# All remaining MLP units ahead of the matrix gathers, with four PSUM bank pairs for each kind of work

## The reference, cut to what matters

```python
x = x + gnn(layernorm(x), W, M, src, dst)          # relu(x@W + segment_sum((x@M)[src], dst))
h = (xn @ W_gat).reshape(M, HEADS, NUM_EXPERTS)    # 16 features a node
a_src = (h * att_src).sum(-1); a_dst = (h * att_dst).sum(-1)
e = leaky_relu(a_src[src] + a_dst[dst], 0.2)
ee = exp(e - segment_max(e, dst)[dst])
agg = segment_sum(h[src] * (ee / segment_sum(ee, dst)[dst])[:, :, None], dst)
g = gates(top2(layernorm(agg)))
out = sum_e g[e] * (gelu(xn @ W1[e] + b1[e]) @ W2[e] + b2[e])
```

## Time and profile before

| | |
|---|---|
| median of 3 runs | 3540.27 us (3537.82 to 3543.89) |
| profiled execution, time | 3540.27 us |
| profiled execution, span | 3539.0 us |
| mean granted TensorE clock | 0.882 of full speed |
| busy: PE, PEld | 2560.6, 1708.4 us |
| busy: DVE, ACT, POOL | 2344.6, 920.5, 2377.0 us |

### The profile page before, as it was taken

The page is one execution under the profiler, slowest core; times in us unless marked ns, Lnnn a source line. Parts: engine busy times, 40 slices in busy tenths (PEclk is TensorE's granted clock), DMA queues, the critical chain, the costliest instruction groups (busy, mean ns, idle before and its releaser), DMA issues.

```text
span 3539.0 us, 36336 instructions
## 1 busy us (share of the span) xinstructions
PE 2560.6 (72%) x10290; PEld 1708.4 (48%) x10315; DVE 2344.6 (66%) x5820; ACT 920.5 (26%) x1581; POOL 2377.0 (67%) x2827
## 2 busy tenths in 40 slices
PE   2556777767677777768877887777798787777725
PEld 1334555545555545546555555555554444443314
DVE  6677676776775555565545555555358898899957
ACT  3000111111112222211111111111145565555514
POOL 3666666666656666646666666666788888888841
PEclk9776998989888989889989888989799999999968
DMA  9676566666666666646666666666622122241147
GB/s 287 227 251 205 180 201 186 204 190 196 203 184 194 205 188 204 201 145 211 202 210 196 200 202 213 197 207 207 171 62 55 45 60 57 55 131 43 41 148 230
DMA packets 476775, 600.78 MB, mean 170 GB/s; under 512 B 72486, under 2 KB 415390, under 8 KB 474526
## 3 DMA queue, kind: packets, MB, share of 16 engines
q1 hardware_dynamic: 378766, 375.94, 32.9%
q0 software_dynamic: 97216, 219.88, 22.4%
q10 hardware_dynamic: 592, 2.64, 0.2%
HBM read 313.06 MB, written 286.79 MB: 169 GB/s over the span
## 4 chain that ended last, share of the span: by engine, by line
DVE 28%; PE 22%; another core or an unknown queue 12%; issue 9%; DMA 3%; ACT 2%; POOL 1%; SPq 0%; DVEq 0%; ACTq 0%; POOLq 0%
PE wide L1535 8%; DVE picked L901 6%; DVE g L905 6%; DVE ring L855 5%; PE wide L1585 4%; PE wide L1595 4%; PE wide L1645 3%; DVE one_hot L788 2%; DMA ring<-xn_d,srci 2%; PE wide L1554 1%; DVE by_row L996 1%; DVE by_row L1003 1%; POOL ring L1737 1%; DVE comb L1178 1%
## 5 line engine op out<-in xcount | busy, mean ns | idle before, releaser
L1737 POOL DMA_INDIRECT ring<-xn_d,srci x1611 | 1562.1, 970 | 907.6 <-issue 415.4
L855 DVE SCALAR_TENSOR_TENSOR ring<-ring,same_v,wide 128x256 f32<-128x256 f32 x1610 | 771.2, 479 | 930.7 <-remote 404.3
L1535 PE MATMUL wide<-ring,one_hot 128*128 128x256 f32 x3222 | 959.1, 435 | 381.8 <-DVE ring L855 194.1
L1535 PEld LDWEIGHTS wide<-ring,one_hot 128*128 128x128 f32 x3222 | 665.4, 216 | 632.0 <-issue 201.1
L1645 PE MATMUL wide<-tab_parts,low_hot 128*128 128x400 bf16 x3144 | 580.9, 339 | 144.6 <-DVE picked L901 102.6
L1789 POOL DMA_INDIRECT g<-tab_d,srt x500 | 496.0, 992 | 82.3 <-POOL pause L1746 49.8
L1645 PEld LDWEIGHTS wide<-tab_parts,low_hot 128*128 128x128 bf16 x3144 | 298.1, 99 | 422.2 <-issue 130.7
L1595 PE MATMUL wide<-w2s,hh 128*128 128x256 f32 x1568 | 413.5, 411 | 46.5 <-DVE yo L829 35.4
L1585 PE MATMUL wide<-xt,w1s 128*128 128x512 f32 (+1 forms) x832 | 420.3, 632 | 21.5 <-ACT hh L1264 13.9
L1264 ACT ACTIVATE hh<-wide,b1c 128x512 f32<-128x512 f32 (+1 forms) x208 | 137.6, 662 | 1000.5 <-PE wide L1585 404.3
L1595 PEld LDWEIGHTS wide<-w2s,hh 128*128 128x128 f32 x1568 | 325.5, 210 | 117.2 <-DVE yo L829 40.0
(11 more groups left out here) (369 smaller groups left out, 1778.0 us busy)
## 6 DMA issues: line engine op xcount, KB each, us to landing
run_d<-ring SPq DMA_DIRECT2D x201, 1024.0 KB
ring<-xn_d,srci POOLq DMA_INDIRECT x1611
y_d<-yo SPq DMA_DIRECT2D x196, 128.0 KB
comb<-y_d SPq DMA_DIRECT2D x28, 896.0 KB
low_row<-low_d SPq DMA_DIRECT2D x13, 1024.0 KB
sum_d<-g SPq DMA_DIRECT2D x15, 768.0 KB
g<-tab_d,srt POOLq DMA_INDIRECT x500
xn_d<-ring SPq DMA_DIRECT2D x7, 896.0 KB, 7.0
```

Source lines behind the costliest of these rows:

```text
L855: dve_at["run", j] = step(V.scalar_tensor_tensor(out=o, in0=ring[:, (j - 1) // JC % RING, (j - 1) % JC, :], scalar=same_v[:, j:j + 1], in1 ...
L1535: mm = T.matmul(bank[pair_bank[p]][:, j % 2 * D:(j % 2 + 1) * D], one_hot[:, j // 4 % 4, j % 4, :], ring[:, j // JC % RING, j % JC, :], st ...
L1737: G.indirect_dma_start(out=ring[:, s, j % JC, :], out_offset=None, in_=xn_d, in_offset=at_rows(srci[:, j:j + 1])).then_inc(sem(f"gather{s} ...
```

## The change

- The seam takes all 56 left units; the matrix steps follow without any unit between them. `turns_2` is one list for all engines, and the `late` shifts are gone.
- For these 56 units, hidden units use the banks 0, 2, 4, 6 in turn and y units 1, 3, 5, 7. A unit waits for the reader of its bank's last content (`bank_free`), not for the reader of the unit before. The units of the first stage keep banks 0 and 1.
- The half blocks use four bank pairs (4, 6, 0, 2) from the start. The first block waits for the last gelu and the last y addition.
- `first_weigh` goes from `TC + 22` (54) to `TC + 12` (44), and `CHUNK_STEPS` from 31 to 32, so the last full chunk ends at step 514 instead of 510.
- `PRELOAD` goes from step 348 to step 40.
- GpSimd's waits: its first 56 gathers follow the y units (14 before), and its waits for picked half blocks are counted from there.

```diff
+HALF_BANK = (4, 6, 0, 2)
-CHUNK_STEPS = 31
+CHUNK_STEPS = 32
...
+    hidden_bank, y_bank, bank_free = [], [], {"hidden": [], "y": []}
+    for u, (what, _, _) in enumerate(units):
+        used = hidden_bank if what == "hidden" else y_bank
+        single, double = (0, (0, 2, 4, 6)) if what == "hidden" else (1, (1, 3, 5, 7))
+        b = single if u < units_1 else double[len(used) % 4]
+        bank_free[what].append(max([k + 1 for k in range(len(used)) if used[k] == b], default=0))
+        used.append(b)
...
+    turns_2 = ["unit"] * left + ["matrix"] * matrix_total
+    first_weigh = TC + 12
...
+    PRELOAD = 40
...
-                    if nl:
-                        T.wait_ge(sem("gelus"), nl)
+                    if bank_free["hidden"][nl]:
+                        T.wait_ge(sem("gelus"), bank_free["hidden"][nl])
...
-                    if ny:
-                        T.wait_ge(dve_step, dve_at["y", ny - 1])
+                    if bank_free["y"][ny]:
+                        T.wait_ge(dve_step, dve_at["y", bank_free["y"][ny] - 1])
...
+                            if b == 0:
+                                T.wait_ge(sem("gelus"), XCH * NX * KF)
+                                T.wait_ge(dve_step, dve_at["y", NT * NX - 1])
                         m = 2 * b + i // 2
-                        if i % 2 == 0 and half_ahead[m] >= 0:
-                            T.wait_ge(dve_step, dve_at["taken", half_ahead[m]])
+                        if i % 2 == 0 and m >= 4:
+                            T.wait_ge(dve_step, dve_at["taken", m - 4])
...
-                if before_it > SEAM_UNITS + LOCK_FREE:
-                    G.wait_ge(sem("picked"), (before_it - SEAM_UNITS - LOCK_FREE) * LOCK_HALVES
-                              // (sum(pool_cols) - SEAM_UNITS) + 1)
+                if before_it > left + LOCK_FREE:
+                    G.wait_ge(sem("picked"), (before_it - left - LOCK_FREE) * LOCK_HALVES // (sum(pool_cols) - left) + 1)
                 pause_once()
-                if before_it < SEAM_UNITS and ahead_of[before_it] > 0:
+                if before_it < left and ahead_of[before_it] > 0:
                     G.wait_ge(sem("y_done"), ahead_of[before_it])
```

More of the change, by code:

```diff
@@ L37 @@
 AHEAD = 2
-SEAM_UNITS = 14
-UNIT_TURNS = 8
-UNIT_FIRST = 4
-ACT_LATE = 6
-DVE_LATE = 6
-SYNC_LATE = 10
+HALF_BANK = (4, 6, 0, 2)
 PAUSE = 280
@@ L435, in build @@
     left = len(units) - units_1
-    spread = [UNIT_FIRST + UNIT_TURNS * k for k in range(left - SEAM_UNITS)]
-    def turns_2(late):
-        turns, waiting = ["unit"] * SEAM_UNITS, list(spread)
-        for n in range(1, matrix_total + 1):
-            turns.append("matrix")
-            while waiting and waiting[0] + late <= n:
-                turns.append("unit")
-                waiting.pop(0)
-        assert not waiting
-        return turns
-    all_banks_from = 2 * (spread[-1] // 4 + 1)
-    half_bank, half_ahead = [], []
-    for m in range(2 * NBLOCKS):
-        free = (4, 6, 2) if m < all_banks_from else (4, 6, 2, 0)
-        used = {b: max([n for n in range(m) if half_bank[n] == b], default=-1) for b in free}
-        b = min(free, key=lambda b: used[b])
-        half_bank.append(b)
-        half_ahead.append(used[b])
-    first_weigh = TC + 22
+    turns_2 = ["unit"] * left + ["matrix"] * matrix_total
+    first_weigh = TC + 12
     weighed_at = {first_weigh + CHUNK_STEPS * c + WEIGH_STEPS: c for c in range(NCF - 1)}
@@ L828, in mlp_units @@
                         V.wait_ge(sem(f"y_out{ny % 4}"), sent(ny // 4 - 1))
-                    dve_at["y", ny] = step(V.tensor_tensor(yo[:, ny % 4, :], bank[Y_BANK][:, 0:D],
+                    dve_at["y", ny] = step(V.tensor_tensor(yo[:, ny % 4, :], bank[y_bank[ny]][:, 0:D],
                                                            b2b[:, jobs[i][1], :], ALU.add))
@@ L899, in pick @@
                 V.wait_ge(dve_step, dve_at["pick", (m - 1) // 2, (m - 1) % 2])
-            first = half_bank[m]
+            first = HALF_BANK[m % 4]
             dve_at["taken", m] = then(V.tensor_tensor(
@@ L1032, in vector_program @@
         table = split_table()
-        for i, turn in enumerate(turns_2(DVE_LATE)):
+        for i, turn in enumerate(turns_2):
             if turn == "unit":
@@ L1343, in scalar_program @@
         done, copies = 0, iter(())
-        for turn in turns_2(ACT_LATE):
+        for turn in turns_2:
             if turn == "unit":
@@ L1581, in mlp_units @@
                         T.wait_ge(sem(f"xt_in{c % 2}"), sent(c // 2))
-                    if nl:
-                        T.wait_ge(sem("gelus"), nl)
+                    if bank_free["hidden"][nl]:
+                        T.wait_ge(sem("gelus"), bank_free["hidden"][nl])
                     for k in range(KD):
-                        mm = T.matmul(bank[HIDDEN_BANK][:, 0:n * P], w1s[:, e, k, f * P:(f + 1) * P],
+                        mm = T.matmul(bank[hidden_bank[nl]][:, 0:n * P], w1s[:, e, k, f * P:(f + 1) * P],
                                       xt[:, c % 2, k, 0:n * P], start=(k == 0), stop=(k == KD - 1))
@@ L1591, in mlp_units @@
                         T.wait_ge(sem("gelus"), KF * (i + 1))
-                    if ny:
-                        T.wait_ge(dve_step, dve_at["y", ny - 1])
+                    if bank_free["y"][ny]:
+                        T.wait_ge(dve_step, dve_at["y", bank_free["y"][ny] - 1])
                     for k in range(KF):
-                        mm = T.matmul(bank[Y_BANK][:, 0:D], hh[:, i % 2, k, f * P:(f + 1) * P], w2s[:, e, k, :],
+                        mm = T.matmul(bank[y_bank[ny]][:, 0:D], hh[:, i % 2, k, f * P:(f + 1) * P], w2s[:, e, k, :],
                                       start=(k == 0), stop=(k == KF - 1))
@@ L1654, in tensor_program @@
         matrix_steps = matrix_gathers()
-        for turn in turns_2(0):
+        for turn in turns_2:
             next(mlp if turn == "unit" else matrix_steps)
@@ L1773, in gpsimd_program @@
                              in_offset=at_rows(smi[:, 4:5])).then_inc(sem("row_in"), 16)
-        ahead_of = [sum(what == "y" for what, _, _ in units[:units_1 + n]) for n in range(SEAM_UNITS)]
+        ahead_of = [sum(what == "y" for what, _, _ in units[:units_1 + n]) for n in range(left)]
         for c in range(NCF):
@@ L1979, in sync_program @@
         done = 0
-        for turn in turns_2(SYNC_LATE):
+        for turn in turns_2:
             if turn == "unit":
```

11 lines of the change are left out of this document (3 added, 8 removed).

## The result

The changed kernel took 3557.51 us (median of 5 runs, 3555.38 to 3572.29) against 3540.27 of the kernel before (5 runs, 3537.82 to 3543.91): a ratio of 1.0066 with a 95% interval of 1.005 to 1.0083, some 23 us slower. The medians of five lie only 17.2 us apart; but 22 executions of the changed kernel are on record, from 3555.38 to 3577.54 us, and their median, 3563.62, is 23.4 us above the old one. The profiled execution took 3575.11 us with a span of 3573.9: it is one of the slowest of the 22.

A forecast was written before the change was run, and what follows sets the result against it. VectorE was taken to set the gathers' pace, starving only while TensorE also does units with three bank pairs. Seam +47.5, gathers -53.8 and remaining waits +9 gave +2.7 us on 3540.27: 3543 us, range 3531 to 3562.

The forecast's parts named there:

- I take 5 us for them: First gathers: VectorE's remaining waits for picks, put at 5 us because TensorE's lead hardly grows there.
- Part 3: Waits that stay in the gathers: 5 us early, 3 later, 1 for the preload; together +9 us, bounds 0 and 34.
- picks' waits above 20 us: Sign of being wrong, in the gathers: waits staying above 20 us, where 6 to 12 us in total were expected.
- GpSimd's last gather past 3375 us: Sign of being wrong, at the end of GpSimd's feature gathers: the last one, at 3360.13 before, moves past 3375.
- Part 1: Seam: 42 units move ahead of the gathers, so these begin at 2645.0 instead of 2597.51: +47.5 us (46 to 51).
- The estimate of 1.6 us: Seam's short units: three y units wait for gelus that short units don't hide, 1.6 us, bounds 0 and 5.
- Part 2: Gathers without units, four bank pairs: first pick to end of logits falls from 786.8 to 733 us, -53.8 us.
- The preload's 1 us: Early gathers: moving the preload of 9 slices to about 2670, into the thin part, costs 1 us of waits.
- Bank depth: Later gathers: four bank pairs hold 8.6 us of picks, three 6.4, so only 3 of 27.8 us of waits stay.
- GpSimd at no cost: GpSimd's feature gathers: 23 us of cover before VectorE's use absorb a seam delay of up to 7 us free.
- the waits stay: Rival, in the gathers: TensorE itself is late, 27.8 us of waits remain, +26 us, 3567; chance 0.31 in part or whole.
- Un-mixing in full: Rival, units moved to the seam: moving them saves only 7.1 us of additions, so +40 us, 3580; chance 0.03.

The follow-up runs named there:

- e4: Changed kernel with the 56 units on banks 0 and 1 alone, as before the change: 3185.61 us, ratio 1.0049 to the kernel before.
- e5: Changed kernel with the preload back at step 348 instead of 40, timed beside a plain copy: 3180.47 us, ratio 1.0015 to the kernel before.
- a1: Changed kernel run again as it is, beside the late-preload version: 3181.09 us, ratio 1.0012 to the kernel before.
- e3: Changed kernel with three bank pairs (4, 6, 2) instead of four for the half blocks: 3173.66 us, ratio 1.0016 to the kernel before.
- b0_before: Kernel before, nothing changed, traced again where its median is 3169.04 us: 816.02 us from the first seam unit to the end of the logits.
- a0_after: Changed kernel run again as it is: 3173.32 us, ratio 1.0017 to the kernel before.
- the fourth set: Later timing set at the slower level, kernel before at 3504.24 us; the plain changed kernel took 3508.02 us, ratio 1.001.
- a2: Changed kernel run again as it is, at the slower level: 3508.02 us, ratio 1.001 to the kernel before.
- the first set: First follow-up timing set, four variants of the changed kernel on one chip, with the kernel before at 3169.10 us.

## Why the prediction was wrong

**The step that failed: "I take 5 us for them", the waits of the first gathers (Part 3).** In the trace that the forecast was for, VectorE waited 28.5 us in the first 22 picks and 0.5 us behind them: 29.0 where the sum has 9. The step rested on the sentence "So VectorE sets the pace, and it starves only while TensorE also does units and has three bank pairs". Here it starved with no unit between the gathers and with four pairs, because TensorE was late by itself: its own idle time stands behind "issue", and VectorE's behind "remote". What slows TensorE there stays open. Term by term, against the first trace of before:

| us | forecast | measured |
|---|---|---|
| seam | +47.5 | +56.3 |
| first pick to the end of the logits | -53.8 + 9 | -23.0 |
| start of the seam | 0 | +1.2 |

The seam's 8.8 us more lie in its short units, behind "issue" and in part at the lower clock. The gathers' 21.8 us more are 20.0 of waits and 1.8 of work. Two of the prediction's own signs of being wrong came: picks' waits above 20 us (29.0), and GpSimd's last gather past 3375 us (3375.82). The forecast range, 3531 to 3562, holds the median of five and not the median of 22 (3563.62) nor the profiled execution. In undisturbed traces the parts come out otherwise, as follows.

**The seam (Part 1): right where TensorE is undisturbed.** The first gather matmul was forecast at start + 81.5 us; undisturbed traces have it at 79.9 to 82.2. Four y banks ended the 3.13 us wait. The estimate of 1.6 us for gelus behind short units was high: 16 matmuls of short units run in 1.95 us, four gelus in 1.77, and only one y unit waited, 0.46 us. The banks for units are the part of the change that pays for itself: without them the seam is 14 us longer (e4).

**The gathers without units (Part 2): right as a time.** 733 us were forecast (735.8 by the first way), 738.2 measured, of which about 1 is waits: 47.9 for the first 22 picks against 48.5, 674.5 for the 15 stretches between resets against 671.5, and 15.8 for the tail as forecast.

**Waits that stay (Part 3), undisturbed: 8 us too high, and wrongly explained.** These copies wait 1 us, not 9. The preload's 1 us was nothing (e5 and a1 do not differ). Bank depth ("four bank pairs hold 8.6 us of picks, three hold 6.4, so of the 27.8 us I keep 3") is not what ended the waits: three pairs without units wait as little (e3), and where units and three pairs stay and TensorE is fed well, 1.3 us are left of the 27.8 (b0_before). The Trainium skill, Perfetto Trace Analysis, section Optimization Strategy, reads a gap that keeps coming back as a possible lack of PSUM buffers, and the prediction said that the trace agreed; e3's 825.5 against 824.8 us says it does not.

**The time of before that the sum starts from.** The prediction took the 56.5 us of waits for a property of the kernel. 23.8 us of TensorE's idle time between 2682 and 3150 were put down to nothing recorded; b0_before shows the same kernel with 13.4 us of picks' waits. The gain from the first pick on is 48.6 us against the first trace (786.8 to 738.2) and 41.9 against b0_before (780.1 to 738.2). And it is another gain: 32.2 of the 41.9 us are waits for GpSimd's features, which the prediction did not have at all.

**GpSimd at no cost.** "These 23 us of cover cost nothing for a delay of up to 32 x 0.2 = 7 us." The size of the delay was met by luck: GpSimd's run grew by 10.3 us, but 9.6 of them lie behind the hold that was to cause it. The cover was not 23 us: against the floor of 16.5 it was 10 in the first trace, and it was there only because VectorE was late. In b0_before it is nothing: there GpSimd sets the end. In the changed kernel the two are so near that either can: a0_after waits for no feature, and its 821.65 us are VectorE's alone (seam 81.2, 2.2 to the first pick, 738.2), 3.1 above GpSimd's floor; a1_after still waits 2.5 us for a feature. So an undisturbed kernel before, in which VectorE waited 32.2 us for GpSimd, could hide most of what the units cost VectorE, and the change puts 47.5 us ahead of the picks and gets 41.9 back: +5.6 us, the difference between 816.0 and 821.65, from one trace of each.

**The sum.** In the three later sets with plain copies the change costs 1.0 to 1.7 parts in a thousand, 3.5 to 5.4 us (in the fourth set the interval includes no change); +2.7 was forecast. From the first pick on the sum had -53.8 + 9 = -44.8 us, and against b0_before -41.9 was measured. That this is near is in part luck: the time of before was 6.7 us too high (786.8 against 780.1), the waits 8 us too high, and VectorE's own work some 4 us too low. On the first chip the change costs 23 us by the ratio. Its profiled execution's seam is 9 us longer than an undisturbed one, and its first 22 picks 26 us (74.1 - 47.9), both with TensorE behind "issue". The rival "the waits stay" came nearest, in its mechanism (TensorE late by itself) and in its sum (32.8 us of waits, 3567 us); but it had 27.8 of them behind the first stretch, where 0.5 are measured. Un-mixing in full (+40) is refuted by every clean copy. By the Trainium skill, Perfetto Trace Analysis, section Optimization Strategy, interleaving regimes may help; the runs agree in the sign, since taking this mixture apart cost time, but the price is some 5 us.

**What stays open.** What slows TensorE's feed. It fills the first stage of every trace of the slower level and of none at the faster one; only in the two traces of the first chip it reaches into the gathers. The preload alone does not make it (a0, a1, a2, e3), and neither do GpSimd's gathers, which run at some 1.5 us in every trace, with a slow feed or without. Whether either makes it worse once it is there was not tested, since no later trace has it in the gathers. That the changed kernel loses more by it is argued, not shown: its slow feed fell on the first gathers, where there is no lead to spend; that of before lay there in part and in part in the middle, where some of it was covered. All 22 executions of the changed kernel there were 15 to 37 us above the old median, so it is no accident of one execution; why the same kernel, in the fourth set at the slower level, is only 0.1% slower, isn't known.

## What to carry to other kernels

Before a gap is explained by buffers or by a neighbour's work, look at what the late engine itself was doing: idle time of TensorE put down to "issue", in groups of one to five matmuls, came and went here with the same schedule, and a sum that starts from such a trace credits the change with what an undisturbed run never had. The cover of a second engine is not the distance from its last instruction to the first use; it is the least distance at any chunk, here the thirteenth, less the 2.4 us that a gather needs to be of use, and it is measured where the engine in front is not late. Where two engines are both busy almost without a pause over the whole stretch (here VectorE 738 us and GpSimd 790), clearing one of them moves only the wait; moving work between them (five wide chunks instead of three) came nearest to a gain, 0.9983 with an interval that reaches 1.0.

## What the hardware showed beyond that

- The kernel before took 3169 to 3174 us in some sets and 3504 to 3540 in others, and one and the same chip was at 3169 in the first set and at 3504 in the fourth. The difference lies in the first stage (start at 2201 to 2215 us against 2536 to 2565 in all traces), with 377.3 us of VectorE's waits for "remote" in a2_after; undisturbed, the second stage takes the same time at both levels (821.65 and 820.3 us).
- In the slow feed groups of matmuls come every 0.73 us (before) or 1.45 us (after) at a granted clock of 1.00 (2787:2791 and 2677:2735).
- Four gelus of 128 columns take 1.77 us in a row; fed slowly they came every 0.75 us, 0.37 us long each.
- One memset and one indirect gather cost GpSimd 1.50 us on average in b0_before and 1.52 in a0_after (from the 57th gather on), with no wait of over 0.2 us between them.
